# A language-model layer on one core: the first attention projection moved into the token loop, its stacks loaded by halves

## The reference

```python
is_hot = hot_mask[flat]
hot_vec = hot_emb_w[tok2hot[flat]]
cold_vec = cold_emb_w[tok2cold[flat]] @ proj_w.T
h = where(is_hot, hot_vec, cold_vec)                     # 2048 x 512

x = layernorm(h)
qkv = einsum('bsd,od->bso', x, w_project)                # 3 x 16 heads x 32
att = softmax(causal(q @ k.T / sqrt(32)))
h = h + (att @ v) @ w_out.T
# then layernorm, router with the best 2 of 16 experts, shared expert, residual
```

## Time and profile before

| | |
|---|---|
| median of 3 runs | 1048.05 us (1047.25 to 1049.69) |
| profiled execution: its own time | 1050.3 us |
| profiled execution: span of the trace | 1048.5 us |
| TensorE busy | 942.9 us (90%) |
| VectorE, ScalarE, GpSimd busy | 667.6, 599.9, 322.1 us |
| mean granted TensorE clock | 0.964 of full speed |

### The profile page before, as it was taken

How to read it: one execution, slowest core, us unless ns; L and a number is a source line. 1 busy time by engine, 2 the same in 40 slices (tenths; PEclk the granted TensorE clock), 3 DMA queues, 4 the chain that set the end, 5 groups by cost and what they waited for, 6 DMA issues and landing times.

```text
span 1048.5 us, 21182 instructions
## 1 busy us (share of the span) xinstructions
PE 942.9 (90%) x6811; PEld 687.2 (66%) x6811; DVE 667.6 (64%) x1746; ACT 599.9 (57%) x1304; POOL 322.1 (31%) x320
## 2 busy tenths in 40 slices
PE   6668599999999999999998899899889899989992
PEld 5324458677686868677685687777766566656661
DVE  8885257565666757566676676668756466656660
ACT  7222177677777777776778622211157677766770
POOL 2286120110202020110202036433233575457642
PEclk9689799999999999999999999899889999999997
DMA  6133733260533334150435111431449577747543
GB/s 213 39 97 95 169 82 82 60 134 1 115 79 82 82 72 93 47 131 17 90 77 200 42 71 61 184 148 51 163 151 335 131 135 166 241 83 135 101 71 41
DMA packets 44574, 114.39 MB, mean 109 GB/s; under 512 B 9332, under 2 KB 11380, under 8 KB 42162
## 3 DMA queue, kind: packets, MB, share of 16 engines
q1 hardware_dynamic: 32146, 87.14, 28.2%
q0 software_dynamic: 12320, 25.90, 13.7%
...
## 4 chain that ended last, share of the span: by engine, by line
PE 54%; DMA 20%; issue 9%; DVE 8%; POOL 4%; ACT 3%; POOLq 1%; DVEq 0%; ACTq 0%
DMA out<-xnT,slot_out 20%; PE psum L527 11%; PE psum L497 8%; PE psum L517 7%; PE psum L540 7%; PE psum L502 5%; PE psum L1259 5%; PE psum L1243 3%; PE psum L1341 2%; PE psum L543 2%; POOL hot_all L1479 1%; DVE oh_lo L1554 1%; ACT probsT L594 1%; DVE oh_hi L1552 1%; PE psum L1284 1%
## 5 line engine op out<-in xcount | busy, mean ns | idle before, releaser
L651 DVE CUSTOM_DVE_ANT_0 psum<-psum,mask_row 128x128 f32<-128x128 f32 (+7 forms) x256 | 194.2, 763 | 58.7 <-PE psum L517 56.3
L609 ACT ACTIVATE probs<-psum,nmax 128x128 f32<-128x128 f32 (+7 forms) x256 | 190.7, 745 | 48.2 <-DVE nmax L651 42.4
L527 PE MATMUL psum<-ident,probs 128*128 128x128 f32 x1152 | 172.6, 275 | 4.7 <-ACT probsT L594 3.3
L517 PE MATMUL psum<-k_stack,q_stack 128*128 128x512 f32 (+2 forms) x384 | 154.9, 458 | 18.7 <-ACT probs L609 9.1
L527 PEld LDWEIGHTS psum<-ident,probs 128*128 128x128 f32 x1152 | 136.1, 140 | 37.1 <-issue 18.6
L594 ACT COPY probsT<-psum 128x512 f32<-128x512 f32 (+3 forms) x256 | 129.3, 505 | 37.7 <-PE psum L527 32.9
L497 PE MATMUL psum<-xnT,w_unit 128*128 128x512 f32 x256 | 131.3, 602 | 0.2 <-ACT full L472 0.2
L873 POOL DMA_INDIRECT out<-xnT,slot_out x47 | 94.3, 2005 | 112.5 <-DMA out<-xnT,slot_out 94.5
L444 POOL CAST part_hi<-full 128x512 fp32r<-128x512 f32 x32 | 19.6, 613 | 351.5 <-ACT full L472 246.8
L517 PEld LDWEIGHTS psum<-k_stack,q_stack 128*128 128x128 f32 x384 | 68.5, 201 | 64.0 <-ACT probs L609 41.0
L1392 PE MATMUL psum<-w_dn,gated_T 128*128 x188 | 88.6, 593 | 1.0 <-ACT gated_T L926 1.0
...
...
## 6 DMA issues: line engine op xcount, KB each, us to landing
...
q_stack<-part_hi SPq DMA_DIRECT2D x64, 128.0 KB, 2.4
q_stack<-part_lo SPq DMA_DIRECT2D x64, 128.0 KB, 2.4
k_stack<-part_hi SPq DMA_DIRECT2D x64, 128.0 KB, 2.4
k_stack<-part_lo SPq DMA_DIRECT2D x64, 128.0 KB, 2.4
...
out<-acc SPq DMA_DIRECT2D x17, 256.0 KB, 2.0
...
```

Of the source, the lines that this page charges most:

```text
L517: mm = pe.matmul(dst[:, c0:c1], qs, k_stack[b][:, h, c0:c1], start=True, stop=True)
L527: mm = pe.transpose(bank(4 + m % 2)[:, (j - 4 * k) * P:(j - 4 * k + 1) * P], probs[n % PSLOTS][:, j * P:(j + 1) * P], ident[:, :])
L609: act.activation(probs[n % PSLOTS][:, 0:(i + 1) * P], bank(2 * (n % 2), 2)[:, 0:(i + 1) * P], ACT.Exp, bias=nmax[:, n % 4:n % 4 + 1], scal ...
L651: dve.tensor_tensor_reduce(out=row, in0=row, in1=mask_row[:, (QT - 1 - i) * P:QT * P], scale=1.0, scalar=3.0e38, op0=ALU.add, op1=ALU.min, ...
```

## The change

The first projection moves from turns 11 to 16 of the token loop to turns 7, 8, 9, 11, 12 and 13, in the order q, k, v of the first 512 tokens and then q, k, v of the second (`FIRST_FILL`). Its copies no longer pass through `full` and GpSimd: ScalarE writes the high part from the bank (`first_high`), VectorE the low part from the bank and the high part (`first_low`), and each next fill waits for that low part (`first_piece`). Five of the 16 look-ups, those of tiles 11 to 15, and the last two batches of row numbers move into turns 1 to 5 of the token loop; look-ups 11, 13 and 15 use bank 7. `LAG` falls from 4 to 2. SyncE issues the stacks of unit 0 by halves of 32 x 512 values: q of the first half behind the h store of tile 7, k of it behind that of tile 8, and both of the second half behind the last h store. The first scores wait for the first half alone, and step 16 for the second. SyncE, ScalarE and VectorE wait for all h stores ahead of their attention part. GpSimd's first split for unit 1 waits for the halves, each for its own.

```diff
@@ -39,11 +39,12 @@
 TILES = TOPK * T // P + E - 1
 WRING = 6
 EARLY_EXPERTS = 4
-LAG = 4
+LAG = 2
+EARLY_LOOKS = 11
+FIRST_FILL = {7: 0, 8: 2, 9: 4, 11: 1, 12: 3, 13: 5}
 SPLIT0 = 5
 SLOT_RING = 6
 SLOT0 = 6
-FILL0 = NT // BATCH + 3
 PSLOTS = 2
 ROUTED_RING = 8
@@ -400,12 +402,22 @@
             sp.dma_start(w_unit[:, :, :], a["wqkv"][g] if isinstance(g, int) else
                          a["wqkv"][bass.ds(g, 1), :, :, :].rearrange("o p k n -> (o p) k n")).then_inc(s_w, 16)
 
-        def stack(sp, u, b, sides=(0, 1), first=False):
-
-            if not first:
-
-                sp.wait_ge(s_S, HEAD + (u - 1) * STEPS)
-            for side in sides:
+        def first_stack(sp, side, half):
+
+            cols = slice(half * 512, half * 512 + 512)
+            st = (q_stack, k_stack)[side][0]
+            sp.wait_ge(s_lo, HEAD + 2 * half + side + 1)
+            for r in range(4):
+                low = r % 2 if side == 0 else r // 2
+                src = part_lo if low else part_hi
+                for h in range(GH):
+                    sp.dma_start(st[32 * r:32 * r + 32, h, cols].bitcast(F32),
+                                 src[32 * h:32 * h + 32, side, cols].bitcast(F32)).then_inc(s_first[half], 16)
+
+        def stack(sp, u, b):
+
+            sp.wait_ge(s_S, HEAD + (u - 1) * STEPS)
+            for side in range(2):
                 st = (q_stack, k_stack)[side][b]
 
                 sp.wait_ge(s_lo, HEAD + 4 * u + 2 * side + 2)
+            return bank(4 if c % 2 == 0 else 5 if c < EARLY_LOOKS else 7)
+
         def passed(pool):
 
             pool.sem_inc(s_passed, 1)
@@ -437,8 +452,9 @@
 
             c = slice(half * 512, half * 512 + 512)
             pool.wait_ge(s_fact if side == 0 else s_fdve, HEAD + 3 * u + half + 1)
-            if loaded is not None:
-
+            if u == 1:
+                pool.wait_ge(s_first[half], STACKED)
+            else:
                 pool.wait_ge(s_stack[1 - b], loaded)
             passed(pool)
             pool.tensor_copy(part_hi[:, side, c], full[:, side, :]).then_inc(s_hi, 1)
...
@@ -484,6 +500,53 @@
                 else:
                     eng.tensor_copy(dst, src).then_inc(s_fdve, 1)
 
+        def first_high(act, c):
+
+            f = FIRST_FILL[c]
+            n = list(FIRST_FILL.values()).index(f)
+            side, half = f // 2, f % 2
+            cols = slice(half * 512, half * 512 + 512)
+            act.wait_ge(s_fill, HEAD + n + 1)
+            if side == 0:
+                act.activation(part_hi[:, 0, cols], bank(7), ACT.Copy, scale=-ATT_SCALE).then_inc(s_hi, 1)
+            elif side == 1:
+                act.copy(part_hi[:, 1, cols], bank(7)).then_inc(s_hi, 1)
+            elif half == 0:
+                act.copy(v_unit[0][:, 0:4, :].rearrange("p a n -> p (a n)"), bank(7)).then_inc(s_fact, 1)
+
+        def first_low(dve, c):
+
+            f = FIRST_FILL[c]
+            n = list(FIRST_FILL.values()).index(f)
+            side, half = f // 2, f % 2
+            cols = slice(half * 512, half * 512 + 512)
+            if side < 2:
+                dve.wait_ge(s_hi, HEAD + 2 * half + side + 1)
+                if side == 0:
+                    dve.scalar_tensor_tensor(out=part_lo[:, 0, cols], in0=bank(7), scalar=-ATT_SCALE,
+                                             in1=part_hi[:, 0, cols].bitcast(F32), op0=ALU.mult,
+                                             op1=ALU.subtract).then_inc(s_lo, 1)
+                else:
+                    dve.tensor_tensor(part_lo[:, 1, cols], bank(7), part_hi[:, 1, cols].bitcast(F32),
+                                      ALU.subtract).then_inc(s_lo, 1)
+            elif half == 1:
+                dve.wait_ge(s_fill, HEAD + n + 1)
+                dve.tensor_copy(v_unit[0][:, 4:8, :].rearrange("p a n -> p (a n)"), bank(7)).then_inc(s_fdve, 1)
+
+        def first_piece(pe, c):
+
+            f = FIRST_FILL[c]
+            pe.wait_ge(s_w, 16)
+            pe.wait_ge(s_xC, 4 * (f % 2) + 4)
+            if f == 0:
+                pe.wait_ge(s_looked, 2 * NT)
+            elif f == 1:
+                pe.wait_ge(s_fact, HEAD + 3)
+            else:
+                pe.wait_ge(s_lo, HEAD + {2: 1, 4: 2, 3: 3, 5: 4}[f])
+            for k in range(KC):
+                fill_products(pe, 0, f, k)
+
         def fill_piece(pe, u, b, f, k, loads):
 
             if k == 0:
...
@@ -546,6 +613,8 @@
             def unit(u, b, g, prev, nxt):
 
                 for n in range(STEPS):
+                    if u == 0 and n + 1 == STEPS // 2:
+                        pe.wait_ge(s_first[1], STACKED)
                     if n + 1 < STEPS:
                         scores(u, b, n + 1)
                     elif nxt:
@@ -564,7 +633,10 @@
 
             def first_scores(u, b, g):
 
-                pe.wait_ge(s_stack[b], STACKED * (g + 1))
+                if u == 0:
+                    pe.wait_ge(s_first[0], STACKED)
+                else:
+                    pe.wait_ge(s_stack[b], STACKED * (g + b))
                 pe.wait_ge(s_fact, HEAD + 3 * u + 3)
                 pe.wait_ge(s_fdve, HEAD + 3 * u + 3)
...
@@ -1424,16 +1496,16 @@
             for c in range(NT):
                 sp.wait_ge(s_h, c + 1)
                 sp.dma_start(h_dram[c * P:(c + 1) * P, :], hot_vec[c][:, :]).then_inc(s_hst, 16)
-                if c == NT - LAG:
-                    stack(sp, 0, 0, (0,), first=True)
-            stack(sp, 0, 0, (1,), first=True)
+                if c in (7, 8):
+                    first_stack(sp, c - 7, 0)
+            for side in range(2):
+                first_stack(sp, side, 1)
+            sp.wait_ge(s_hst, 16 * NT)
             att_sp(sp)
             moe_sp(sp)
 
         @block.gpsimd
         def _(pool):
-            for s in (s_lo, s_hi):
-                pool.sem_inc(s, HEAD)
             pool.memset(xn[:, 0, :], 0.0).then_inc(s_zeros, 1)
             for m, v in ((ident, 0.0), (ident_bf, 0.0), (tri_bf, 1.0), (mask_row, 0.0)):
                 pool.memset(m[:, :], v).then_inc(s_pool, 1)
...
-                    split_part(pool, 0, 0, half // 2, half % 2, None)
             att_pool(pool)
             moe_pool(pool)
 
         @block.scalar
         def _(act):
-            for s in (s_E, s_Ca, s_fact, s_ZR):
+            for s in (s_E, s_Ca, s_fact, s_ZR, s_hi):
                 act.sem_inc(s, HEAD)
+            act.sem_inc(s_fact, 2)
             act.wait_ge(s_const, 9)
             act.wait_ge(s_ratio, 1)
 
@@ -1519,15 +1588,17 @@
                     act.wait_ge(s_xT, t + 1)
                     act.copy(xnT[:, :, t * P:(t + 1) * P],
                              bank(2 + t % 2).rearrange("p (k n) -> p k n", k=KC)).then_inc(s_xC, 1)
-                if 0 <= c - FILL0 < FILLS:
-                    fill_evac(act, "act", 0, c - FILL0, 0)
+                if c in FIRST_FILL:
+                    first_high(act, c)
+            act.wait_ge(s_hst, 16 * NT)
             att_act(act)
             moe_act(act)
 
         @block.vector
         def _(dve):
-            for s in (s_M, s_Cd, s_Zr, s_Z, s_AT, s_fdve):
+            for s in (s_M, s_Cd, s_Zr, s_Z, s_AT, s_fdve, s_lo):
                 dve.sem_inc(s, HEAD)
+            dve.sem_inc(s_fdve, 2)
             step = Chain(dve, s_dve)
             dve.wait_ge(s_const, 5)
             step(dve.reciprocal(row_over_chunk[:, :], chunk1[:, :]))
@@ -1620,17 +1691,22 @@
                 dve.tensor_scalar(xn[:, s, :], hot_vec[c][:, :], mv[:, s, 0:1], rstd[:, s:s + 1],
                                   ALU.subtract, ALU.mult).then_inc(s_xn, 1)
 
-            for k in range(BATCHES):
-                for c in range(k * PER, (k + 1) * PER):
-                    look_up(c)
-                row_numbers(k)
+            for c in range(EARLY_LOOKS):
+                look_up(c)
+                if c % PER == PER - 1:
+                    row_numbers(c // PER)
             for c in range(NT + 1):
+                if c in FIRST_FILL:
+                    first_low(dve, c)
                 if c < NT:
                     embed(c)
                 if c >= 1:
                     norm(c - 1)
-                if 0 <= c + 1 - FILL0 < FILLS:
-                    fill_evac(dve, "dve", 0, c + 1 - FILL0, 0)
+                if 1 <= c <= NT - EARLY_LOOKS:
+                    look_up(EARLY_LOOKS + c - 1)
+                    if (EARLY_LOOKS + c) % PER == 0:
+                        row_numbers((EARLY_LOOKS + c) // PER - 1)
+            dve.wait_ge(s_hst, 16 * NT)
             att_dve(dve)
             moe_dve(dve)
 
@@ -1658,15 +1734,18 @@
                       stop=True).then_inc(s_base, 1)
             pe.wait_ge(s_tab, 1)
             pe.wait_ge(s_tohC, 2)
-            for c in range(NT):
+            def look(c):
                 if c >= 2:
                     pe.wait_ge(s_looked, 2 * (c - 1))
-                b = bank(4 + c % 2)
+                b = look_bank(c)
                 oh = tok_ohT[:, c, :]
```

(12 more changed lines are left out.)

18 lines of the change are left out of this document (10 added, 8 removed).

## The result

The changed kernel took 1037.01 us in the median of 4 runs (1034.81 to 1038.05), the kernel before beside it 1047.65: a ratio of 0.9889, with a 95% interval of 0.987 to 0.9909. Repeated on two chips it gave 0.9864 (0.9841 to 0.9888) and 0.989 (0.9849 to 0.9931). The forecast was 1034.8, in a range of 1031.5 to 1040.0. The profiled execution took 1038.05 us, its span 1036.3 against 1048.5 before: 12.2 us less. The medians are 10.6 us apart here, and 14.3 and 10.4 in the two repeats.

The account below looks back on a forecast made before the run. Ahead of attention, issuing of stacks behind the last h store was taken as the bound, with `xnT` behind it. First scores 12.3 us earlier plus 1.0 for the clock, 13.3 off the 1048.05 median, gave 1034.8 us, range 1031.5 to 1040.0.

Parts of the forecast that it names:

- The low part: VectorE's low part in the fills' hand-over, not in the trace: taken as 0.7 us, with 0.6 and 1.3 as ends.
- The term that was wrong: the clock: Granted clock at the start of unit 0: 1.0 us gain taken, between 2.1 if full and nothing if fallen.
- the full branch: Clock stays full into unit 0: slow pairs cost 1.02 instead of 1.91 us, 2.1 us gained in all.
- One sign of being wrong: Profile after: a PEclk of 0.50 behind 72 us would show the forecast wrong.
- one of the variants of the forecast: Near variants, clock full or fallen at the first scores: 1033.5 to 1036.5 us, chance 0.60 together with the forecast.
- The pace of tiles 3 to 5: Token loop turns with a look-up: VectorE sets the pace, 3.06 us a turn.
- The slack of 1.2 to 3.3 at step 16: Second half stacks seen by TensorE at 133.2, step 16 at 136.5, or 134.4 with full clock.
- The clock was not low in the fills: Rival: half clock lasts into the fills, costing 3.4 to 5 us, 1038.3 to 1040 us; chance 0.14.
- The gathers were not late: Rival: gathers of late tiles land late beside stacks, tiles 12 to 15 some 2 us late, 1037 us; chance 0.08.
- Step 16 did not wait: Rival: step 16 waits for the second half, up to 1 us, 1035.8, up to 3 with hiccups; chance 0.07.
- The hand-over was not long: Rival: VectorE's hand-over between fills is longer, low part 1.3 us, costing 2.4 us, 1037.2 us; chance 0.06.
- A half did not cost what a large transfer does: Slower rival: each half costs SyncE 1.08 us, step 16 is 20 us late, 1055 us; chance 0.03.

Follow-up runs that it names:

- busy tail: Changed kernel plus matmuls whose result nobody reads, in turns 16 to 18: 1032.68 us, ratio to before 0.9852; second time 1031.19 us, 0.9856.
- second half delayed: Changed kernel plus sixteen 256 KB stores on SyncE ahead of the second half stacks: 1045.22 us, ratio to the kernel before 1.0005.

## Why the prediction held

**The mechanism, point by point.** Predicted and measured in the profile after: h of tile 0 52.8 and 52.50; first fill 72.2 and 71.39; sixth fill 100.2 and 99.65; h of tile 15 109.6 and 108.89; first scores 114.2 and 114.01; first half issued 98.9 and 98.20; second half issued 131.0 and 131.00. Two of these agree by luck. The second half began 0.8 us earlier than worked out (109.96 for 110.8), and its last sixteen transfers took 0.69 us each instead of 0.63. And h of tile 1 came 1.4 us early, of which later turns that were longer than worked out took back more than half: h of tile 6 was forecast for 73.2 and came at 72.61. No wait on a stack was left. The low part, which no row before showed, took 0.69 (0.7 taken); the rows of VectorE stand below.

**The term that was wrong: the clock.** I took 1.0, between 0 for a fallen clock and 2.1 for a full one. The size of the full branch was right: 22.14 us (mean of three) from first scores to step 16 against 19.94 with a full clock, 2.2. But the clock fell in every profile of the changed kernel, and the term was 0 (22.67 us in the profile after, 22.32 before). The step that failed is this middle value, drawn from two stretches before that pointed to different ends. One with TensorE busy 0.50 of 2.00 had kept the clock, and it was given as much weight as the fall behind 116; in the tail the clock fell in a stretch with 0.77 of 2.00. A busy share of a single stretch doesn't decide it. One sign of being wrong came true with it: PEclk was 0.50 behind 72 us. The sign was meant for the fills, but it was written without that limit, though a clock fallen in the tail was one of the variants of the forecast. Without the 1.0 the forecast is 1035.8, and what remains to 1037.01 is within the runs' range.

**Smaller misses.** h of tile 1 was forecast for 55.6 and came at 54.24, because the clock rose at 53. The kernel's work doesn't fix that instant: with the same work until then, it came at 54.36, 54.68, 54.81 and 55.12 in other executions. The pace of tiles 3 to 5 was 3.17 us, not 3.06: a normalization took 0.72 there, and 0.55 from tile 6 on.

```profile
66.56 0.72 DVE L1691 TENSOR_SCALAR xn<-hot_all,mv,rstd 128x512 f32<-128x512 f32 x1
...
74.36 0.55 DVE L1691 TENSOR_SCALAR xn<-hot_all,mv,rstd 128x512 f32<-128x512 f32 x1
75.72 0.69 DVE L526 SCALAR_TENSOR_TENSOR part_lo<-psum,part_hi 128x512 fp32r<-128x512 f32 x1 [0.82 <-ACT part_hi L511]
...
80.89 0.69 DVE L530 TENSOR_TENSOR part_lo<-psum,part_hi 128x512 fp32r<-128x512 f32 x1 [2.27 <-issue]
```

The slack of 1.2 to 3.3 at step 16 was measured as 4.2: the last half, begun at about 130.4, landed in 2.0 rather than 2.4 us and was there at 132.4 rather than 133.2, and with the low clock step 16 stood at 136.68. GpSimd's second split, which waits for the same half, began at 132.56. With the clock full, step 16 at 134.17 to 134.64 leaves about 2. Another date was missed without a price: the k stacks of unit 1 were issued by 162.2, not 156, still 10 us ahead of its first scores.

**The rivals.** The clock was not low in the fills: 1.00 from 54 us. In others it rose up to two us later, and in three of them, whose programs are the same until turn 16, it fell once more (from 62 to 64 us 0.56 and 0.50 with the busy tail, and 0.50 with the second half delayed), but was back at 1.00 ahead of the fills. The rival's condition thus occurred in the early turns, but not its price. The gathers were not late: they landed in 3.3 us as before. Step 16 did not wait. The hand-over was not long. A half did not cost what a large transfer does. Here stands what the Trainium skill says ("DMA: Bandwidth & Descriptors", Rules for kernel authors: under 64 KB mostly overhead is paid): in SyncE's queue the trace goes beyond it, as 64 and 128 KB both cost 0.63 us. The rule speaks against the change and is right on the price; the change wins nonetheless, since 32 of the 64 transfers lie beside tiles.

**Off by how much.** In the profile, 12.2 us gained of 13.3 forecast: 12.5 for 12.3 at the first scores, 0 for 1.0 by the clock, and 0.3 lost up to step 16. Between the medians it is 10.6 gained of 13.3.
